# A transformer block on one core: GpSimd's additions cut by tile, the last stage's second products and the first attention's statistics moved

## The chip, the cores and the metric

The kernel runs on one core of a Trainium2 chip. Its engines are TensorE (PE, with its weight loads as PEld), VectorE (DVE), ScalarE (ACT), GpSimd (POOL) and SyncE (SP, which issues DMAs here). The metric is the device time of one execution in microseconds; the time of a kernel is the median of its runs.

## What is computed

x is 4 x 1024 tokens of 256 features (worked on as 8 halves of 4 tiles of 128 tokens; a context of 154 tokens for each of 4 batch rows, `ctx_1024`, gives keys and values). Four residual parts follow each other:

```python
x = x + tanh(g_xattn[0]) * xattn_0(layernorm(x), ctx)   # 16 heads, projections, stablemax, bias
x = x + tanh(g_ffn[0])   * moe(layernorm(x))            # 64 experts, top 8, capacity 128, and a shared expert
x = x + tanh(g_xattn[1]) * xattn_1(layernorm(x), ctx, ctx)   # softmax, no projections
x = x + tanh(g_ffn[1])   * ffn_1(layernorm(x))          # butterfly layers around a GELU

# stablemax: s = where(x >= 0, x + 1, 1 / (1 - x)); s / sum(s)
# ffn_1, whose butterflies the kernel folds into its two weight matrices:
h = butterfly(x @ W_exp + b_exp, up_weights)
h = gelu(h + up_bias)
y = butterfly(h, down_weights) @ W_con + b_con + down_bias
```

## The kernel before, in words

x stays in SBUF for the whole program, as [128 tokens, 32 tiles, 256 features]; `half_of(h)` is a half's four tiles (4 x 256 = 1024 elements a partition). Products that need precision are made of three products of split parts (a high part and a rest: `feats`, `hidden`, `w_up_high`/`w_up_low`, `w_con_high`/`w_con_low`).

The order of the work is a plan: a list of units such as `("out", h, b, k)`. Each engine walks the same list and emits the instructions that it has for each unit (`units[...]`), so the list sets each engine's order; semaphores set when an instruction may start. There are three stages.

- First attention, `plan_first`. Score products (L797, L799, L800) and the weighing of values (L816, L821) of one half run chunk by chunk with the stablemax of ACT (L1156, L1160, L1164) and DVE (L1488). What follows a half's attention is cut into steps by `after_steps(h)` and put between the chunks of the next half, one step for each chunk: division, transposing the result (`turn_att`, PE L851), `att_feats` (ACT's copies of it out of PSUM into `row_feats`, L1125), `project_o` (bias L862, products L867), `x_add` (DVE L1509: x += gate * product), statistics of the next norm (DVE L1363, POOL L1873 and L1878), norm, transposing, gate and top 8.
- The experts. Their sums come back by indirect DMA and by `fetch` in 512 KB pieces; POOL adds them to x (`add_experts`, L1910).
- Last stage, `plan_last`. It has 20 places c for each of the 8 halves, and a ninth round (h == 8) with no attention of its own. In round h the second attention of half h runs (scores L797, exponentials L1299, weighing, transposes L1068, DVE L1789 to L1794: x += gate * attention) and `beside(h, c)` says what of half h-1's last feed-forward part stands at place c: the norm "f" at c = 2 and 5 (DVE L1363, L1372, L1408; POOL L1873, L1878), `bias_out` at 7 (POOL L1914: x += the output bias), `turn_f` at 8 (PE L743; ACT L1125 and DVE L1814 make `feats`), and two bursts b = 0 and 1 at c = 9 and 13. A burst is four `up` units (PE L1085, 6 matmuls each; ACT's GELU L1328 into `hidden_whole`, of which there are two; DVE's cast L1822 and POOL's subtraction L1920 split it) and four `out` units k at c, c+1, c+2 and c+3 (PE L1100, 12 matmuls each, into two PSUM banks). Behind k = 3 stands DVE's `out_add` (L1834, two instructions of 512 elements): x += gate * products. `beside(h, 6)` also has `add_experts` for half h+2, and score maxima (`peak`, PE L1032, DVE L1774) of later halves run in between.

`out_biased` counts the bias additions, `out_added` the instructions of `out_add` (four a half), `hid_split` the subtractions. Before the change, DVE's `out_add` of burst 0 waits for `out_biased`. Exponential and GELU have different tables on ACT; a change of table is an ACT_TABLE_LOAD.

Of the kernel before, what the change touches and what calls it, by code (L numbers as in the profile page):

```python
# [14 lines left out]
ALU = mybir.AluOpType  # L15
# [3 lines left out]
P = 128  # L19
BATCH, SEQ, DIM = 4, 1024, 256  # L20
# [150 lines left out]

def after_steps(h):
    turn, divide = [("normalize", h, t) for t in range(HT)], [("divide", h, t) for t in range(HT)]
    return [turn[0:2], divide[0:2] + turn[2:4], divide[2:4], [("turn_att", h)], [("att_feats", h)],
            [("project_o", h, 0), ("project_o", h, 1)], [("x_add", h, 0), ("x_add", h, 1)],
            [("stats", "r", h), ("rstd", "r", h)], [], [("norm", "r", h)], [("turn_rows", h)], [("row_feats", h)],
            [("gate", h)], [("shift", h)], [("gate_exp", h)], [("top", h)], [("pick", h)], [("pick_rows", h), ("count", h)],
            [("position", h)]]

# [157 lines left out]

BURST_AT = (9, 13)


def peak_units(h, c):

# [5 lines left out]
def burst(h, b, peak):  # L348

    up = [("up", h, BURST * b + k) for k in range(BURST)]  # L350
    peak = peak + [None] * (4 - len(peak))
    units = [up[0], up[1], peak[0], up[2], peak[1], up[3], peak[2], ("out", h, b, 0), peak[3]]
    return [u for u in units if u]


def beside(h, c):


    units, peak = [], []
    if h + 1 < HALVES:  # L360
        peak += peak_units(h + 1, c)
    if h + 2 < HALVES:
        peak += peak_units(h + 2, c - PER_HALF)
        if c == 0:
            units.append(("fetch", h + 2))
        if c == 6:
            units += [("add_experts", h + 2, i) for i in range(SUMS)]
        if c == 10:
            units += norm_units("q1", h + 2)[:2]
        if c == 11:  # L370
            units += norm_units("q1", h + 2)[2:]
        if c == 12:
            units.append(("turn_q1", h + 2))
        if c == 13:
            units += [("send_q1", h + 2, 0), ("send_q1", h + 2, 1)]
        if c in (16, 19):
            units.append(("send_q1", h + 2, 2 + c // 19))
    if h % 2 == 0 and h + 2 < HALVES:
        b = h // 2 + 1
        if c == 1:  # L380
            units += [("load_k1", b, 0), ("load_k1", b, 1)]
            if h:
                units.append(("load_v1", b))
        if c in KEYS_AT:
            n = KEYS_AT.index(c)
            units.append(("key_split1", b, n))
            if n < 2:
                units.append(("load_k1", b, n + 2))
    if 1 <= h <= HALVES:
        if c == 2:  # L390
            units += norm_units("f", h - 1)[:2]
        if c == 5:
            units.append(norm_units("f", h - 1)[2])
        if c == 7:
            units.append(("bias_out", h - 1))
        if c == 8:
            units.append(("turn_f", h - 1))
        for b, at in enumerate(BURST_AT):
            if c == at:
                return units + burst(h - 1, b, peak)  # L400
            if at < c < at + BURST:
                units.append(("out", h - 1, b, c - at))
    return units + peak


# [68 lines left out]
def build(nc, D, out):  # L474
    ctx = ExitStack()
    with ctx:
# [882 lines left out]
        def vector_program(V):  # L1359
# [464 lines left out]
            def out_add(h, b, k):  # L1824
                if k == BURST - 1:
                    n = 2 * h + b
                    if b == 0:
                        V.wait_ge(out_biased, h + 1)
                    V.wait_ge(out_made, BURST * (n + 1))
                    for two in range(HT // 2):  # L1830
                        xs = x[:, HT * h + 2 * two:HT * h + 2 * two + 2, :].rearrange("p i f -> p (i f)")
                        if b:
                            V.wait_ge(out_added, 2 * n - 1 + two)
                        V.scalar_tensor_tensor(xs, out_bank[two], tg[:, 3:4], xs, ALU.mult,  # L1834
                                               ALU.add).then_inc(out_added, 1)
# [21 lines left out]
        def gpsimd_program(G):  # L1857
# [43 lines left out]
            def add_experts(h, i):  # L1901
                if h:
                    G.wait_ge(fetched_in[i], 16 * h)
                    if h >= HALVES - LATE:
                        G.wait_ge(*late.freed(("sh_down", h, 1)))
                    if i:
                        G.wait_ge(x_added, SUMS * (h - 1) + i)
                    elif h == 1:
                        G.wait_ge(keys_split, BATCH + 4)
                    G.tensor_tensor(half_of(h), half_of(h), fetched[i][:, :, :], ALU.add).then_inc(x_added, 1)  # L1910

            def bias_out(h):
                G.wait_ge(ln_normed, HT * (norm_no["f", h] + 1))
                G.tensor_tensor(half_of(h), half_of(h), b_out[:, :].unsqueeze(1).to_broadcast([P, HT, DIM]),  # L1914
                                ALU.add).then_inc(out_biased, 1)

            def hidden_rest(h, k):
                n = HB * h + k
# [361 lines left out]
```

## Time and profile before

| | |
|---|---|
| median of 3 runs | 1219.74 us (1217.71 to 1219.98) |
| the profiled execution | 1221.16 us, span 1219.4 us, mean granted clock 0.929 |
| busy, share of the span | PE 85%, PEld 62%, DVE 67%, ACT 58%, POOL 29% |
| chain that ended last | PE 50%, DVE 25%, ACT 11%, issue 5%, DMA 3%, POOL 3% |
| costliest parts of the chain | PE L914 6%, L1100 6%, L1085 5%, L930 4%, L1003 4%; DVE L1363 3% |

"Span" is the part of the execution that the trace covers. A granted clock of 1.00 is 2.4 GHz for TensorE, one of 0.50 is 1.2 GHz. In a row of the timeline, the number in brackets is the engine's idle time ahead of the instruction and what ended it. The first attention runs from about 40 to 350 us, the experts until about 770, the last stage from there to the end.

### The profile page before, as it was taken

What the parts mean: (1) busy time and instruction counts of PE and PEld (TensorE: products, weight loads), DVE (VectorE), ACT (ScalarE), POOL (GpSimd) and SP (SyncE); (2) the same over time, 40 slices, a digit from 0 to 9 for tenths busy, and PEclk for the clock granted to TensorE, in tenths of its full rate; (3) what the DMA queues carried; (4) which work ended last, traced back from release to release, by engine and by line L of the source; (5) the groups of instructions that cost most, each with busy time, mean ns of one, the idle gap of its engine ahead of it and who ended that gap; (6) DMA issues with size and microseconds to landing.
All of it is one profiled execution on the core that took longest, in us unless ns stands there. A gap on an engine that the chain in (4) does not pass through costs nothing.

```text
span 1219.4 us, 17480 instructions
## 1 busy us (share of the span) xinstructions
PE 1032.5 (85%) x5635; PEld 752.1 (62%) x5635; DVE 812.7 (67%) x2053; ACT 702.0 (58%) x1351; POOL 356.6 (29%) x313
## 2 busy tenths in 40 slices
PE   3888888788876788999899977889898989999878
PEld 2444544454434677877688756657676766767657
DVE  4668777877787756755657566786677677665443
ACT  2999988888965424564654431365554545444532
POOL 2000000000000003777767721233424152523223
PEclk9898988988878889999999995799999999999988
DMA  6645435442121423888888653331322233110000
GB/s 157 177 91 169 121 94 148 141 119 73 53 108 35 147 91 84 185 210 212 227 191 182 142 137 74 98 97 26 107 55 72 61 90 97 37 48 1 20 18 18
DMA packets 97435, 128.42 MB, mean 105 GB/s; under 512 B 27009, under 2 KB 69377, under 8 KB 97089
## 3 DMA queue, kind: packets, MB, share of 16 engines
q1 hardware_dynamic: 82960, 106.32, 30.6%
q0 software_dynamic: 12288, 18.88, 8.7%
q10 hardware_dynamic: 2096, 2.10, 0.8%
q8 instruction: 46, 0.75, 0.3%
q14 instruction: 45, 0.36, 0.1%
HBM read 66.15 MB, written 30.70 MB: 79 GB/s over the span
## 4 chain that ended last, share of the span: by engine, by line
PE 50%; DVE 25%; ACT 11%; issue 5%; DMA 3%; POOL 3%; SPq 2%; ACTq 1%; DVEq 0%; POOLq 0%
PE psum L914 6%; PE psum L1100 6%; PE psum L1085 5%; PE psum L930 4%; PE psum L1003 4%; DVE stats L1363 3%; PE psum L821 3%; PE psum L797 3%; PE psum L867 3%; PE psum L1032 2%; DVE weights L1488 2%; DVE peaks L1774 2%; PE psum L743 2%; ACT weights L1160 2%; PE psum L962 2%
## 5 line engine op out<-in xcount | busy, mean ns | idle before, releaser
L1873 POOL TENSOR_SCALAR vareps<-moments 128x4 f32<-128x4 f32 x32 | 10.4, 324 | 509.8 <-DVE moments L1372 509.8
L797 PE MATMUL psum<-q_stack,k_stack 96*128 96x512 f32 (+1 forms) x256 | 122.6, 508 | 33.2 <-DVE weights L1488 19.0
L1299 ACT ACTIVATE weights<-psum 128x512 f32<-128x512 f32 x160 | 94.0, 596 | 72.5 <-PE psum L797 61.1
L1488 DVE SCALAR_TENSOR_TENSOR weights<-psum,weights 128x512 f32<-128x512 f32 x160 | 102.6, 681 | 37.8 <-ACT weights L1164 37.6
L1893 POOL DMA_INDIRECT expert_sums<-made,sum_rows x64 | 103.2, 1613 | 61.5 <-DVE made L1738 37.7
L1032 PE MATMUL psum<-k_stack,q_stack 96*128 96x256 f32 x256 | 88.4, 397 | 33.0 <-DVE peaks L1774 21.5
L1920 POOL TENSOR_TENSOR hidden<-hidden_whole,hidden 128x512 fp32r<-128x512 f32 x64 | 82.2, 1286 | 115.9 <-DVE hidden L1822 115.9
L1774 DVE TENSOR_REDUCE peaks<-psum 128x2 f32<-128x308 f32 x256 | 107.2, 470 | 11.4 <-PE psum L1034 11.0
L914 PE MATMUL psum<-feat_parts,w_shared_up 128*128 128x512 f32 x384 | 99.1, 408 | 7.2 <-ACT shared_silu L1211 2.8
L1100 PE MATMUL psum<-w_con_high,hidden 128*128 128x256 f32 x512 | 101.7, 297 | 0.0
L1822 DVE CAST hidden<-hidden_whole 128x512 fp32r<-128x512 f32 x64 | 50.3, 787 | 73.8 <-ACT hidden_whole L1328 72.6
L1885 POOL DMA_INDIRECT got<-rows_scratch,tokens x64 | 68.3, 1067 | 97.1 <-DVE sum_rows L1725 77.9
L1156 ACT ACTIVATE weights<-psum 128x512 f32<-128x512 f32 x160 | 88.7, 596 | 11.4 <-PE psum L797 11.4
L1160 ACT ACTIVATE weights<-weights 128x512 f32<-128x512 f32 x160 | 94.1, 635 | 1.0
L1164 ACT ACTIVATE weights<-weights 128x512 f32<-128x512 f32 x160 | 93.9, 632 | 1.0
L797 PEld LDWEIGHTS psum<-q_stack,k_stack 96*128 96x128 f32 (+1 forms) x256 | 50.3, 201 | 71.1 <-issue 41.0
L1085 PE MATMUL psum<-feats,w_up_high 128*128 128x512 f32 x256 | 83.0, 423 | 11.6 <-DVE feats L1814 6.6
L1032 PEld LDWEIGHTS psum<-k_stack,q_stack 96*128 96x128 f32 x256 | 53.5, 209 | 61.1 <-DVE peaks L1774 28.6
L1100 PEld LDWEIGHTS psum<-w_con_high,hidden 128*128 128x128 f32 x512 | 80.9, 190 | 13.8 <-POOL hidden L1920 6.8
L914 PEld LDWEIGHTS psum<-feat_parts,w_shared_up 128*128 128x128 f32 x384 | 72.2, 194 | 23.3 <-DVE shared_silu L1612 3.6
L1328 ACT ACTIVATE hidden_whole<-psum,hidden_bias 128x512 f32<-128x512 f32 x64 | 42.7, 686 | 64.8 <-PE psum L1085 58.0
L1003 PEld LDWEIGHTS psum<-got_t,expert_w 128*128 128x128 f32 x512 | 64.2, 191 | 25.4 <-ACT got_t L1263 18.1
(211 smaller groups left out, 2416.2 us busy)
## 6 DMA issues: line engine op xcount, KB each, us to landing
expert_w<-in_expert_w SPq DMA_DIRECT2D x64, 384.0 KB, 4.2
q_stack<-q_stage SPq DMA_DIRECT2D x96, 128.0 KB, 2.9
q_stack<-q_stage SPq DMA_DIRECT2D x174, 64.0 KB, 2.0
expert_sums<-zeros SPq DMA_DIRECT2D x6, 1408.0 KB, 8.3
fetched<-expert_sums SPq DMA_DIRECT2D x14, 512.0 KB, 4.7
rows_scratch<-rows SPq DMA_DIRECT2D x8, 640.0 KB, 3.4
k_raw<-in_k SPq DMA_DIRECT2D x16, 300.0 KB
x<-in_x SPq DMA_DIRECT2D x8, 512.0 KB, 4.9
```

Of the source, the lines that this page charges most:

```text
L797: T.matmul(to, k[0:row, head_at(head), :], q[0:row, head // 2, :], start=True, stop=True).then_inc(scored, 1)
L914: m = T.matmul(shared_banks(h).ap(key, half), w_sgu[:, pw, a:a + P], sh_parts[:, pf, c * HALF:(c + 1) * HALF], start=n == 0 and c == 0, st ...
L1003: m = T.matmul(bank[2][:, part * P:(part + 1) * P], expert_w[e % 8][:, c, part * INNER:(part + 1) * INNER], got_t[e % 3][:, c, :], start=c ...
L1032: T.matmul(view[:, :, 0:P], q[0:STACK, p, t * P:(t + 1) * P], keys[0:STACK, 2 * p:2 * p + 2, :], start=True, stop=True)
L1085: m = T.matmul(wide.ap(key), up_parts[pw][:, c, k * P:(k + 1) * P], feats[:, pf, c, :], start=i == 0 and c == 0, stop=i == 2 and c == CD - 1)
L1100: m = T.matmul(out_bank[t // 2][:, t % 2 * DIM:(t % 2 + 1) * DIM], hidden[k][:, ph, t * P:(t + 1) * P], con_parts[pw][:, BURST * b + k, :] ...
L1160: A.activation(weights[n % 9][:, :], weights[n % 9][:, :], ACT.Ln, bias=1.0).then_inc(logged, 1)
L1164: A.activation(weights[n % 9][:, :], weights[n % 9][:, :], ACT.Exp, scale=-1.0).then_inc(exped, 1)
L1299: A.activation(weights1[n % 6][:, :], score_bank[n % 2], ACT.Exp).then_inc(exped, 1)
L1488: V.scalar_tensor_tensor(weights[n % 9][:, :], score_bank[n % 5], 1.0, weights[n % 9][:, :], ALU.add, ALU.max).then_inc(weighted, 1)
L1774: V.tensor_reduce(peaks[h % 2][:, t, 2 * p:2 * p + 2], view, AX.X, ALU.max).then_inc(wide.frees(key, i), 1)
L1893: G.indirect_dma_start(sum_dram[e % SUMS], bass.IndirectOffsetOnAxis(ap=sum_rows[:, e:e + 1], axis=0), made[e % 4][:, :], None, bounds_che ...
```

## The change

Four things are changed.

1. POOL's additions to x, of the experts' sums and of the output bias, are made tile by tile: four instructions of 128x256 for each of 128x1024. The semaphore is counted once, by the last of the four.
2. `bias_out` moves from c = 7, where it waited for the norm, to c = 12, where it waits for both instructions of `out_add` of the first burst. `out_add` of the second burst now waits for it, and that of the first no longer does.
3. The second burst's `out` units of half 6, (6, 1), are kept out of round 7's places 13 to 16 and put at places 2, 2, 5 and 5 of the ninth round, behind the norm units of those places.
4. `after_steps`: an empty step comes before `att_feats`, and `x_add` and the statistics of the norm become one step, so everything behind keeps its place.

```diff
-    return [turn[0:2], divide[0:2] + turn[2:4], divide[2:4], [("turn_att", h)], [("att_feats", h)],
-            [("project_o", h, 0), ("project_o", h, 1)], [("x_add", h, 0), ("x_add", h, 1)],
-            [("stats", "r", h), ("rstd", "r", h)], [], [("norm", "r", h)], [("turn_rows", h)], [("row_feats", h)],
+    return [turn[0:2], divide[0:2] + turn[2:4], divide[2:4], [("turn_att", h)], [], [("att_feats", h)],
+            [("project_o", h, 0), ("project_o", h, 1)],
+            [("x_add", h, 0), ("x_add", h, 1), ("stats", "r", h), ("rstd", "r", h)], [], [("norm", "r", h)], [("turn_rows", h)], [("row_feats", h)],
...
+KEPT_BACK, KEPT_BACK_AT = (HALVES - 2, 1), (2, 2, 5, 5)
...
-    units = [up[0], up[1], peak[0], up[2], peak[1], up[3], peak[2], ("out", h, b, 0), peak[3]]
+    first = None if (h, b) == KEPT_BACK else ("out", h, b, 0)
+    units = [up[0], up[1], peak[0], up[2], peak[1], up[3], peak[2], first, peak[3]]
...
-        if c == 7:
+        if c == 12:
             units.append(("bias_out", h - 1))
...
-            if at < c < at + BURST:
+            if at < c < at + BURST and (h - 1, b) != KEPT_BACK:
                 units.append(("out", h - 1, b, c - at))
+        if h == HALVES:
+            units += [("out", *KEPT_BACK, k) for k in range(BURST) if c == KEPT_BACK_AT[k]]
...
-                    if b == 0:
+                    if b:
                         V.wait_ge(out_biased, h + 1)
...
-                    G.tensor_tensor(half_of(h), half_of(h), fetched[i][:, :, :], ALU.add).then_inc(x_added, 1)
+                    for t in range(HT):
+                        xt = x[:, HT * h + t, :]
+                        m = G.tensor_tensor(xt, xt, fetched[i][:, t, :], ALU.add)
+                    m.then_inc(x_added, 1)

             def bias_out(h):
-                G.wait_ge(ln_normed, HT * (norm_no["f", h] + 1))
-                G.tensor_tensor(half_of(h), half_of(h), b_out[:, :].unsqueeze(1).to_broadcast([P, HT, DIM]),
-                                ALU.add).then_inc(out_biased, 1)
+                G.wait_ge(out_added, 4 * h + 2)
+                for t in range(HT):
+                    xt = x[:, HT * h + t, :]
+                    m = G.tensor_tensor(xt, xt, b_out[:, :], ALU.add)
+                m.then_inc(out_biased, 1)
```

The changed program's lines are numbered 5 higher up to the additions, and 10 to 16 higher behind them. Its order on the engines differs at these places.

PE, first attention, around one half's `project_o` (L862 and L867, after the change L867 and L872), before:

```order
L816 MATMUL psum<-weights,values 128x512
L851 MATMUL psum<-ident,att 128x128 x8
L797 MATMUL psum<-q_stack,k_stack 128x512 x2
L862 MATMUL psum<-bias_parts,bias_ones 128x512
L867 MATMUL psum<-wo,row_feats 128x256 x4
L862 MATMUL psum<-bias_parts,bias_ones 128x512
L867 MATMUL psum<-wo,row_feats 128x256 x4
L797 MATMUL psum<-q_stack,k_stack 128x512 x2
L821 MATMUL psum<-weights,values 32x512 x4
L799 MATMUL psum<-q_stack,k_stack 128x512
L800 MATMUL psum<-q_stack,k_stack 128x512
```

and after:

```order
L821 MATMUL psum<-weights,values 128x512
L856 MATMUL psum<-ident,att 128x128 x8
L802 MATMUL psum<-q_stack,k_stack 128x512 x4
L826 MATMUL psum<-weights,values 32x512 x4
L867 MATMUL psum<-bias_parts,bias_ones 128x512
L872 MATMUL psum<-wo,row_feats 128x256 x4
L867 MATMUL psum<-bias_parts,bias_ones 128x512
L872 MATMUL psum<-wo,row_feats 128x256 x4
L804 MATMUL psum<-q_stack,k_stack 128x512
L805 MATMUL psum<-q_stack,k_stack 128x512
L821 MATMUL psum<-weights,values 128x512
L802 MATMUL psum<-q_stack,k_stack 128x512 x2
```

The four score products stand together, and with the four weighing products in front of `project_o`, where two score products stood before.

POOL, last stage, around one half's bias addition, before:

```order
L1920 TENSOR_TENSOR hidden<-hidden_whole,hidden 128x512 x4
L1873 TENSOR_SCALAR vareps<-moments 128x4
L1878 TENSOR_TENSOR rstd<-vareps,minus_half 128x4
L1914 TENSOR_TENSOR x<-x,bias_out 128x1024
L1920 TENSOR_TENSOR hidden<-hidden_whole,hidden 128x512 x8
```

and after:

```order
L1878 TENSOR_SCALAR vareps<-moments 128x4
L1883 TENSOR_TENSOR rstd<-vareps,minus_half 128x4
L1930 TENSOR_TENSOR hidden<-hidden_whole,hidden 128x512 x4
L1924 TENSOR_TENSOR x<-x,bias_out 128x256 x4
L1930 TENSOR_TENSOR hidden<-hidden_whole,hidden 128x512 x4
```

The addition leaves the place behind the reciprocal deviation (L1878) for the one between the two bursts' subtractions.

DVE, from the last attention's `x` updates of half 7 to `feats`, before:

```order
L1834 SCALAR_TENSOR_TENSOR x<-psum,tanh_gates,x 128x512 x2
L1789 RECIPROCAL sums_0<-psum 128x16
L1791 TENSOR_TENSOR att_0<-psum,sums_0 128x256
L1794 SCALAR_TENSOR_TENSOR x<-att_0,tanh_gates,x 128x4x64
L1789 RECIPROCAL sums_1<-psum 128x16
L1791 TENSOR_TENSOR att_1<-psum,sums_1 128x256
L1794 SCALAR_TENSOR_TENSOR x<-att_1,tanh_gates,x 128x4x64
L1363 BN_STATS stats<-x 128x6 x4
L1372 BN_AGGR moments<-stats 128x2 x4
L1408 TENSOR_SCALAR normed<-x,moments,rstd 128x256 x4
L1814 TENSOR_TENSOR feats<-psum,feats 128x512 x2
```

and after:

```order
L1827 CAST hidden<-hidden_whole 128x512 x4
L1794 RECIPROCAL sums_0<-psum 128x16
L1796 TENSOR_TENSOR att_0<-psum,sums_0 128x256
L1799 SCALAR_TENSOR_TENSOR x<-att_0,tanh_gates,x 128x4x64
L1794 RECIPROCAL sums_1<-psum 128x16
L1796 TENSOR_TENSOR att_1<-psum,sums_1 128x256
L1799 SCALAR_TENSOR_TENSOR x<-att_1,tanh_gates,x 128x4x64
L1368 BN_STATS stats<-x 128x6 x4
L1377 BN_AGGR moments<-stats 128x2 x4
L1413 TENSOR_SCALAR normed<-x,moments,rstd 128x256 x4
L1839 SCALAR_TENSOR_TENSOR x<-psum,tanh_gates,x 128x512 x2
L1819 TENSOR_TENSOR feats<-psum,feats 128x512 x2
```

The update of x by (6, 1) (L1834, L1839) moves behind the last normalisation. On PE the 48 products of (6, 1) move likewise: they now stand between the last transposes of the attention (L1068, L1073) and those of `turn_f` (L743, L748).

## Rows read from the trace of the kernel before

**Rows 1.** Windows: stretch, length, busy time of each engine (instructions), clock.

```profile
779.00:793.00 14.00, 13.21 (x50) 8.66 (x48) 10.46 (x28) 5.52 (x10) 2.10 (x3) 0.51 0.22 38
...
1182.00:1196.00 14.00, 8.53 (x23) 6.48 (x24) 5.00 (x16) 3.85 (x5) 4.37 (x4) 0.51 0.00 0
```

**Rows 2.** Waits, first attention: engine, line <- line: total, times, longest us.

```profile
ACT row_feats L1125 <- PE psum L851: 14.6, 5, 3.6
```

**Rows 3.** POOL's groups: count, busy us, mean ns, idle before and releasers.

```profile
L1878 POOL TENSOR_TENSOR rstd<-vareps,minus_half 128x4 f32<-128x4 f32 x32 | 33.2, 1037 | 4.6
L1910 POOL TENSOR_TENSOR x<-x,fetched 128x1024 f32<-128x1024 f32 x14 | 33.2, 2370 | 53.2 <-DMA fetched<-expert_sums 43.7 <-DVE k_stack L1758 8.5 <-POOL x L1910 0.2
```

**Rows 4.** Timeline, half 6: start, us, engine, line, [idle before].

```profile
1142.65 2.38 POOL L1914 TENSOR_TENSOR x<-x,bias_out 128x1024 f32<-128x1024 f32 x1 [1.57 <-DVE normed L1408]
...
1143.24 2.08 DVE L1794 SCALAR_TENSOR_TENSOR x<-att,tanh_gates,x 128x256 f32<-128x256 f32 x1
...
1146.62 0.70 PE L1085 MATMUL psum<-feats,w_up_high 128*128 128x512 f32 x2 [2.00 <-DVE feats L1814]
```

**Rows 5.** Timeline, half 5, the same place.

```profile
1093.62 1.29 DVE L1814 TENSOR_TENSOR feats<-psum,feats 128x512 fp32r<-128x512 f32 x2 [0.36 <-ACT feats L1125]
...
1095.01 0.47 PE L1085 MATMUL psum<-feats,w_up_high 128*128 128x512 f32 x1 [0.45 <-issue]
```

**Rows 6.** Chain of waits, last two halves: start, us, what.

```profile
1146.62 7.36 PE psum L1085 x24
...
1189.67 8.62 PE psum L1085 x24
...
1203.98 5.55 PE psum L1085 x24
1209.54 5.70 PE psum L1100 x48
```

**Rows 7.** Timeline, half 2.

```profile
930.09 0.70 PE L1085 MATMUL psum<-feats,w_up_high 128*128 128x512 f32 x2 [1.51 <-DVE feats L1814]
```

**Rows 8.** Timeline, ahead of the last stage's halves, DVE.

```profile
775.54 2.37 DVE L1794 SCALAR_TENSOR_TENSOR x<-att,tanh_gates,x 128x256 f32<-128x256 f32 x1
```

**Rows 9.** Timeline, half 0, POOL and DVE.

```profile
814.33 4.93 POOL L1910 TENSOR_TENSOR x<-x,fetched 128x1024 f32<-128x1024 f32 x2 [4.39 <-DMA fetched<-expert_sums]
...
819.22 2.57 POOL L1914 TENSOR_TENSOR x<-x,bias_out 128x1024 f32<-128x1024 f32 x1
...
819.79 2.28 DVE L1822 CAST hidden<-hidden_whole 128x512 fp32r<-128x512 f32 x1 [0.24 <-ACT hidden_whole L1328]
```

**Rows 10.** Timeline, half 0, between the two bursts.

```profile
839.16 1.40 DVE L1834 SCALAR_TENSOR_TENSOR x<-psum,tanh_gates,x 128x512 f32<-128x512 f32 x2
...
842.54 1.28 POOL L1920 TENSOR_TENSOR hidden<-hidden_whole,hidden 128x512 fp32r<-128x512 f32 x1 [8.27 <-DVE hidden L1822]
...
844.38 0.69 ACT L1328 ACTIVATE hidden_whole<-psum,hidden_bias 128x512 f32<-128x512 f32 x1 [1.87 <-PE psum L1085]
```

**Rows 11.** Timeline, half 7, between the two bursts.

```profile
1204.09 1.41 DVE L1834 SCALAR_TENSOR_TENSOR x<-psum,tanh_gates,x 128x512 f32<-128x512 f32 x2 [3.98 <-PE psum L1100]
...
1206.78 1.29 POOL L1920 TENSOR_TENSOR hidden<-hidden_whole,hidden 128x512 fp32r<-128x512 f32 x1 [5.30 <-DVE hidden L1822]
...
1211.73 1.29 POOL L1920 TENSOR_TENSOR hidden<-hidden_whole,hidden 128x512 fp32r<-128x512 f32 x1 [0.36 <-DVE hidden L1822]
```

**Rows 12.** Timeline, first attention, half 0, ACT.

```profile
86.21 1.09 ACT L1156 ACTIVATE weights<-psum 128x512 f32<-128x512 f32 x2 [1.62 <-PE psum L797]
```

**Rows 13.** Timeline, first attention, PE and ACT beside one row_feats.

```profile
205.68 1.16 PE L816 MATMUL psum<-weights,values 128*128 128x512 f32 x2
...
207.40 1.08 ACT L1125 ACTIVATE row_feats<-psum 128x512 f32<-128x512 f32 x2 [3.37 <-PE psum L851]
```

**Rows 14.** Timeline, PE ahead of the last transposes.

```profile
1186.01 2.21 PE L743 MATMUL psum<-ident,normed 128*128 128x128 f32 x8 [5.16 <-DVE normed L1408]
```

**Rows 15.** Timeline, ACT in the last attention.

```profile
1169.87 1.28 ACT L1299 ACT_TABLE_LOAD   x1
```

## The prediction

> **What bounds the kernel now.** I read the busy shares first: PE 85% of the span, DVE 67%, ACT 58%, POOL 29%, with the granted clock at 9 tenths in most slices. So PE is the engine to feed, and POOL's own time counts only where somebody waits for it. Then I took the stretches in which the clock falls to half. The reader should see two long ones, 14 us each, at clock 0.51 [rows 1]: one behind the first additions of the last stage, one around the last normalisation. Then the timeline just ahead of each, to find who was late. In both, and in most short stalls of that stage, the chain is: POOL works on x with 128x1024 elements, DVE's small update of x stretches beside it, the split of `feats` comes late, PE's `up` products come late. In the first attention I read the table of waits; there the one row on this change is ACT's wait for the transposes that it copies, 14.6 us in 5 times [rows 2].
>
> The profiled execution took 1221.16 us (span 1219.4), 1.4 above the median of the runs, 1219.74. I sum against 1221.2 and subtract 1.4 at the end.
>
> **A. The additions by tile (14 by experts, 8 of the bias): gain 9.5.** An addition of 1024 elements takes 2.37 us [rows 3]. In half 6, the bias addition ran from 1142.65 to 1145.03; DVE's 256-element update started at 1143.24 and took 2.08 us, to its end [rows 4]. Where nothing of POOL's lies beside it the same form takes some 0.48. The engine that starts first keeps the other waiting until its instruction ends. So PE's `up` started after 2.00 us idle [rows 4], against 0.45 in half 5, where DVE had 0.36 to spare [rows 5]: 1.55. Its 24 matmuls then took 7.36 us, where 24 at full clock take about 5.55 [rows 6]; 1.8 more, of which I take 1.45, since a slice of the clock's fall may remain. Half 6 gives 3.0. In three earlier halves the addition of experts meets the same update; PE's idle time there was 1.51 [rows 7], and 1.69 and 0.54 in the same row of the next two: 1.1 + 1.2 + 0.1 = 2.4. At 775.54 the update took 2.37, 1.9 more than alone [rows 8], and the half-clock stretch [rows 1] follows: 1.9 and, of the clock, 1.0, as much of these 14 us is bound by DVE (busy 10.46): 2.9. At 814 two additions (4.93) and the bias addition behind them (2.57, from 819.22) hold POOL, and DVE's cast takes 2.28 [rows 9] where it takes 0.43 alone. Afterwards eight slices (5.95) and two casts between them (0.86) take 6.8 against 7.5, 0.7, with 0.5 for the clock behind it: 1.2.
>
> What a slice costs is not in the trace. POOL's 128x512 form takes 1.28 to 1.29 [rows 10, 11], its 1024 form 2.37: 1.08 for 512 elements and 0.20 fixed, so 0.20 + 0.54 = 0.74 for 256. The bounds are 0.59 (a quarter of 2.37) and 1.29 (not below the 512 form); I take 0.74. Four slices are 2.98, 0.6 longer than one addition, but DVE can get between two of them, and then waits 0.74 at most and 0.37 on average, about the 0.36 it can spare.
>
> The row of 1143.24 shows a block, not a slowing of both. The Trainium skill, "SBUF — State Buffer", section "Who interferes with whom", says the same: DVE and GpSimd share a port pair, and the first to issue holds it for its whole instruction. Its rule speaks against the change too, as the lock works both ways: DVE's casts between two slices hold up POOL. By that the four bias slices would take up to 2.98 + 3 x 0.43 = 4.3; this is the price used under B, which rests on the rows of the casts.
>
> **B. The bias addition behind the first burst's update: loss 5.9.** It leaves the place before `turn_f` and waits for DVE's update by the first burst; POOL then cannot start the second burst's subtractions. The gap between that update's end and the first subtraction is its cover. The first of the eight, half 0: 840.56 to 842.54, 1.98 [rows 10]. The last, half 7: 1205.50 to 1206.78, 1.28 [rows 11]. Between them, by the same two rows of each half, 2.0, 3.0, 2.0, 3.0, 3.0, 3.0. The bias needs 3.0 and a start of 0.1, and a cast (0.43) gets in now and then. Three halves at 2.0: 3.1 + 0.5 - 2.0 = 1.6 late. The third GELU of half 0 started at 844.38 for PE, while the subtraction that frees its buffer had ended at 843.82 [rows 10], so 0.56 is hidden; 1.0 to 1.1 each, 3.3. Halves at 3.0: 0.25 each for three, 0.75; half 6, where the exponentials of the last attention queue behind the GELUs, 0.65. Half 7: POOL 1.9 late; the fourth subtraction would end at 1214.9 instead of 1213.02 [rows 11], and PE wants it for the last 12 of the 48 products that start at 1209.54 and take 5.70 [rows 6], at 1209.54 + 3 x 1.43 = 1213.8: 1.2. Sum 5.9. Bounds: 0, if PE's other work covers all; and 8 x 3.1 = 24.8, if the gaps are filled by nothing useful and the addition stands on the path in full. I stay near the rows with gaps. DVE's second update now waits for the bias, but its products end many us later; nothing.
>
> **C. First attention: gain 1.9.** Per half, two score products more and four of the weighing come ahead of `project_o`. ACT fed by them no longer idles 1.62 us ahead of 86.21 [rows 12]: 1.6 in half 0. In the other halves, ACT copies `row_feats` one clip later, and its wait ends with the weighing at 206.84 (205.68 + 1.16) instead of at the copy, 207.40 [rows 13]: 0.5 sooner, but `project_o` and so DVE's x_add and statistics come some 1.2 us later, and the next transposes take most of it back; 0.05 each, 0.3. Bounds: 14.6 if the whole row of waits goes [rows 2]; -3.5 if in seven halves the later statistics cost 0.5 each. I stay near the lower part, because PE (busy 85%) must do the same products.
>
> **D. The tail: gain 3.5.** 48 `out` products of half 6 leave the last attention groups. There they took four pieces of 1.43 or more; now they stand in PE's idle 5.16 us [rows 14] before `turn_f`. Without them the attention is bound by ACT, whose table load starts at 1169.87 [rows 15], and ends about 1.65 sooner (six exponentials and two copies at 0.6, then the last weighing, 2.1, and its copy: 1178.5 against 1180.14). The moved products then run from 1179.2 to 1184.9, and `turn_f` starts there instead of at 1186.01: 1.1 sooner. PE doesn't cool: the 24 matmuls at 8.62 [rows 6] cost 5.55, 3.1 more. That makes 4.2; I take 3.5, as the thinner attention tail may cost some clock. Bounds: 4.2, and -1 if the products run at the clock of the 14 us at 0.51 [rows 1]. DVE's update of (6, 1) moves behind the normalisation, where DVE is idle; nothing.
>
> **Sum.** 9.5 - 5.9 + 1.9 + 3.5 = 9.0; 1221.2 - 9.0 = 1212.2; less 1.4, 1210.8, told as 1211.
>
> **Rivals.**
> 1. *C is larger.* ACT's waits in the first attention go by half, 7.3 instead of 1.9: about 5.5 more, 1205.5. For it: the wait is one cause in 5 places. Against: PE has the same work there.
> 2. *The tail cools.* Taking 48 products out of the last attention thins PE's work; the clock falls there, the moved products take up to twice 5.7 us and `turn_f` is late. D goes from 3.5 to about -0.5: 1215. For it: PE fell to 0.51 in this very stretch [rows 1]. The Trainium skill, "TensorE: Matmul & The Clock Gate", section "HAM oscillation — how this bites in real kernels", describes short pieces of matmuls between waits that run cold each time; it would make this rival the forecast.
> 3. *Stalls change hands.* DVE waits for slices four times where it waited once, A shrinks to about 2: 1218.5, within the bound of no change.
> 4. *Slower: the slice.* 32 bias slices stand behind the first burst's update, in gaps that are full. Each us that a slice costs beyond 0.74 adds up to 32 us; 9 us of gain are gone at 0.74 + 9/32 = 1.0. At 1.2 (near the 128x512 row) 14.7 are lost: 1226. For it: POOL's 128x4 form of the same kind takes 1.04 [rows 3], so the fixed part may depend on operands. Against: two sizes of plain additions give 0.20 fixed.
>
> **Chances.** Forecast 0.50 (its own range 1207.5 to 1214.5); rival 1 0.14; rival 2 0.16; rival 3 0.09; rival 4 0.11. About 0.2% (2.4 us) is what a measurement of this kernel tells from no change. Forecast, rival 1, and nearly all of rival 2 are faster: 0.78; rival 3 and a rest of 2 are the same: 0.13; rival 4, less a little, slower: 0.09. The range 1204.5 to 1219 takes in rivals 1 to 3 and leaves out 4 and the far ends of C.
>
> **What would show it.** A: DVE's update of x never over 1.2 us in the last stage, PE's idle before `up` about 0.5; slices near 0.74. B: between update and first subtraction 3.0 to 3.6 us in each half. C: the wait of ACT at 86 gone. D: no idle over 2 us before the last `turn_f`, and the next 24 matmuls in 5.6. The forecast is wrong if slices take 1 us or more, if the clock in the last 50 us stays near half, or if halves 0, 1 and 3 of the last stage grow by more than 2 us each.

## The result

| | before | after |
|---|---|---|
| median | 1219.86 us (1217.71 to 1222.35, 4 runs) | 1237.83 us (1236.55 to 1238.79, 4 runs) |
| profiled execution's span | 1219.4 us | 1236.0 us |
| mean granted clock | 0.929 | 0.911 |

The changed kernel is slower: ratio 1.0127, interval 1.0100 to 1.0154. The forecast was 1211 us, range 1204.5 to 1219. It was wrong in sign.

### The profile page after: what moved, and what is told of

Its sections match the earlier page's. It is cut to its first block, busy times and chain, and to the rows that moved or that the text cites. A ratio compares the mean times of both kernels' runs of the same rounds, so it can differ in the third digit from the quotient of the medians.

```text
span 1236.0 us, 17538 instructions
## 1 busy us (share of the span) xinstructions
PE 1052.7 (85%) x5635; PEld 765.1 (62%) x5635; DVE 801.9 (65%) x2053; ACT 702.9 (57%) x1351; POOL 371.0 (30%) x379
## 4 chain that ended last, share of the span: by engine, by line
PE 54%; DVE 24%; ACT 9%; issue 5%; POOL 3%; SPq 2%; DMA 2%; ACTq 1%; DVEq 0%; POOLq 0%
PE psum L919 6%; PE psum L1105 5%; PE psum L1090 5%; PE psum L1008 4%; PE psum L826 4%; PE psum L935 4%; PE psum L802 4%; DVE stats L1368 3%; PE psum L872 3%; DVE weights L1493 3%; DVE peaks L1779 2%; PE psum L748 2%; PE psum L821 2%; PE psum L1037 2%; PE psum L967 2%
## 5 line engine op out<-in xcount | busy, mean ns | idle before, releaser
L1878 POOL TENSOR_SCALAR vareps<-moments 128x4 f32<-128x4 f32 x32 | 10.4, 324 | 526.5 <-DVE moments L1377 526.5
L802 PE MATMUL psum<-q_stack,k_stack 96*128 96x512 f32 (+1 forms) x256 | 125.9, 525 | 47.1 <-DVE weights L1493 30.4
L1827 DVE CAST hidden<-hidden_whole 128x512 fp32r<-128x512 f32 x64 | 45.2, 711 | 80.7 <-ACT hidden_whole L1333 79.6
L1090 PE MATMUL psum<-feats,w_up_high 128*128 128x512 f32 x256 | 80.2, 410 | 13.6 <-ACT hidden_whole L1333 8.7
L1008 PEld LDWEIGHTS psum<-got_t,expert_w 128*128 128x128 f32 x512 | 66.8, 198 | 24.6 <-ACT got_t L1268 14.8
L826 PE MATMUL psum<-weights,values 128*32 128x512 f32 x512 | 80.9, 707 | 1.1 <-ACT turned L1176 1.1
```

The costliest lines, as they stand in the source:

```text
L802: T.matmul(to, k[0:row, head_at(head), :], q[0:row, head // 2, :], start=True, stop=True).then_inc(scored, 1)
L826: m = T.matmul(to[32 * j:32 * j + 32, :], vals[:, 0, 4 * g + j, :], w[(n + j) % len(w)][:, :], start=True, stop=False, tile_position=(0, 3 ...
L1008: m = T.matmul(bank[2][:, part * P:(part + 1) * P], expert_w[e % 8][:, c, part * INNER:(part + 1) * INNER], got_t[e % 3][:, c, :], start=c ...
L1090: m = T.matmul(wide.ap(key), up_parts[pw][:, c, k * P:(k + 1) * P], feats[:, pf, c, :], start=i == 0 and c == 0, stop=i == 2 and c == CD - 1)
```

## The profile after

First, where the time went. I cut both traces at instructions that both have: the reciprocal deviations of the norms, which POOL computes (L1878, after the change L1883). The 16th, at the end of the first attention, starts at 375.1 us before and at 393.6 after: 18.5 late. The 18th, shortly ahead of the last stage, is 21.3 late; the end of the span 16.6. So the last stage gained 4.7, the forecast's A, B and D together, and the loss is in the first attention, the forecast's smallest term. (The other 2.8 us between the two cuts are in the experts' stage, whose length differs between the traces of all kernels by 6 us.) The lateness grows from half to half, at the deviations of the norm behind each half's attention: 0.9, 4.0, 5.4, 6.6, 11.3, 12.9, 15.3 and 18.5.

The stretch from 40 us to that deviation by the windows (length, then busy time of PE, PEld, DVE, ACT, POOL with instructions, granted clock, DMA share, GB/s). Before:

```profile
40.00:375.10 335.10, 279.02 (x1274) 155.35 (x1272) 256.82 (x735) 289.72 (x559) 16.78 (x28) 0.90 0.40 112
```

After:

```profile
40.00:393.70 353.70, 297.37 (x1279) 166.90 (x1278) 258.08 (x735) 291.05 (x559) 16.86 (x28) 0.84 0.38 106
```

Subtract the busy time from the length. PE's idle time is 335.1 - 279.0 = 56.1 before and 353.7 - 297.4 = 56.3 after. It did not wait longer; it was busy 18.4 us longer with the same instructions. DVE and ACT did the same work within 1.4 us of the same time. What changed is the clock, 0.90 to 0.84. In windows of half a microsecond, PE was at 1.2 GHz (a clock under 0.75) for 68 us before and 110 after; by my estimate 42 us more at half speed cost about 21 us, near the 18.4. In six traces with the old steps (before, e1, e5, e6, e9, f1) this time is 58 to 73.5 us and PE's busy time 275.8 to 283.3, so the change stands clear of the scatter.

The wait that the prediction counted on [rows 2] did go, and another came. Waits from 40 to 350 us, the stretch of [rows 2], before:

```profile
PE psum L797 <- DVE weights L1488: 19.0, 18, 2.2
```

and after:

```profile
PE psum L802 <- DVE weights L1493: 28.6, 23, 2.2
...
ACT turned L1176 <- PE psum L821: 21.4, 10, 3.3
DVE x L1514 <- PE psum L872: 18.4, 13, 1.7
```

ACT's 14.6 us for `row_feats` are not in the answer any more; its wait for the weighing, 4.5 us in 4 times before, is 21.4 in 10. Much of it is the same idle time under the name of the next instruction in the queue, as half 3 shows. After, against [rows 13]:

```profile
210.84 1.02 PE L821 MATMUL psum<-weights,values 128*128 128x512 f32 x2
211.70 1.03 PE L856 MATMUL psum<-ident,att 128*128 128x128 f32 x8
211.96 0.60 ACT L1176 ACTIVATE turned<-psum 128x512 f32<-128x512 f32 x1 [2.48 <-PE psum L821]
```

ACT starts 1.12 us behind the start of the weighing, where it was 1.72: 0.6 sooner, as forecast (0.5); its idle time fell from 3.37 to 2.48. What follows a few microseconds behind that place is shown by half 2, before:

```profile
172.50 1.07 PE L821 MATMUL psum<-weights,values 128*32 128x512 f32 x8
...
174.54 1.25 DVE L1488 SCALAR_TENSOR_TENSOR weights<-psum,weights 128x512 f32<-128x512 f32 x2
...
175.25 1.10 PE L797 MATMUL psum<-q_stack,k_stack 96*128 96x512 f32 x2 [0.17 <-DVE weights L1488]
```

and after:

```profile
177.59 0.75 DVE L1514 SCALAR_TENSOR_TENSOR x<-psum,tanh_gates,x 128x512 f32<-128x512 f32 x1 [1.60 <-PE psum L872]
...
178.38 1.40 DVE L1368 BATCH_NORM_STATS2 stats<-x 128x6 f32<-128x256 f32 x4
...
179.98 1.26 DVE L1493 SCALAR_TENSOR_TENSOR weights<-psum,weights 128x512 f32<-128x512 f32 x2
...
180.69 1.09 PE L802 MATMUL psum<-q_stack,k_stack 96*128 96x512 f32 x2 [1.82 <-DVE weights L1493]
...
182.26 2.20 PE L748 MATMUL psum<-ident,rows 128*128 128x128 f32 x8 [0.47 <-DVE rows L1413]
```

DVE did the same in this piece before as after: its second x_add, the statistics and the weights follow each other, and the weights start 2.39 us behind the x_add (172.15 to 174.54, and 177.59 to 179.98). PE's next scores overwrite what the weights read, so they wait for them. What changed is PE's own work beside that: two scores and the weighing of the row at 172.50, about 1.7 us, stood behind `project_o` before and have been pulled in front of it. PE idles 1.82 us where it idled 0.17 before. The transposes of the norm, 1.64 us in the same place before, take 2.20. The windows show the fall. Before, at the same place:

```profile
176.00:180.00 4.00, 3.43 (x19) 1.51 (x19) 3.74 (x10) 3.94 (x9) 0.12 (x1) 1.00 0.00 0
```

and after:

```profile
174.00:178.00 4.00, 4.00 (x18) 3.06 (x17) 1.27 (x3) 4.00 (x9) 0.00 (x0) 1.00 0.00 0
178.00:182.00 4.00, 1.87 (x5) 0.41 (x3) 3.50 (x12) 3.94 (x8) 1.26 (x2) 1.00 0.00 0
182.00:186.00 4.00, 3.74 (x14) 2.10 (x18) 4.00 (x15) 2.85 (x6) 0.04 (x1) 0.65 0.04 12
```

Four full microseconds, four with PE busy for 1.87, then a clock of 0.65. Half 0 shows the exchange in small: ACT's idle 1.62 [rows 12] is gone, and PE pays 1.81 behind it:

```profile
85.79 1.07 ACT L1161 ACTIVATE weights<-psum 128x512 f32<-128x512 f32 x2
...
89.92 1.10 PE L802 MATMUL psum<-q_stack,k_stack 96*128 96x512 f32 x2 [1.81 <-DVE weights L1493]
```

The last stage went mostly as forecast. The slices, against [rows 3]:

```profile
L1917 POOL TENSOR_TENSOR x<-x,fetched 128x256 f32<-128x256 f32 x56 | 40.1, 746 | 49.0 <-DMA fetched<-expert_sums 39.5 <-DVE k_stack L1763 8.5 <-POOL x L1917 0.2
...
L1924 POOL TENSOR_TENSOR x<-x,bias_out 128x256 f32<-128x256 f32 x32 | 25.4, 824 | 45.4 <-DVE x L1839 45.4
```

0.746 us for a slice, forecast 0.74; those of the bias take 0.82, with DVE's casts beside them. Half 6 without its stall, against [rows 4]:

```profile
1164.16 0.48 DVE L1799 SCALAR_TENSOR_TENSOR x<-att,tanh_gates,x 128x256 f32<-128x256 f32 x1
1166.00 0.70 PE L1090 MATMUL psum<-feats,w_up_high 128*128 128x512 f32 x2 [0.45 <-issue]
```

And the last two halves by the chain of waits, against [rows 6]:

```profile
1166.00 5.79 PE psum L1090 x24
...
1206.53 7.34 PE psum L1090 x24
```

7.36 became 5.79, 8.62 became 7.34. The moved bias in half 7, against [rows 11]:

```profile
1219.61 1.41 DVE L1839 SCALAR_TENSOR_TENSOR x<-psum,tanh_gates,x 128x512 f32<-128x512 f32 x2 [3.18 <-PE psum L1105]
...
1221.10 3.19 POOL L1924 TENSOR_TENSOR x<-x,bias_out 128x256 f32<-128x256 f32 x4 [3.29 <-DVE x L1839]
...
1224.26 2.52 POOL L1930 TENSOR_TENSOR hidden<-hidden_whole,hidden 128x512 fp32r<-128x512 f32 x2
```

The first subtraction starts 3.24 us behind the update's end, 1.28 before. Over the eight halves these gaps are 3.01, 4.05, 3.25, 4.05, 3.25, 3.23, 3.26 and 3.24, where they were 1.98, 2.00, 3.01, 2.01, 3.01, 2.99, 3.00 and 1.28. Two of them lie above the 3.0 to 3.6 that the prediction gave for each half.

## The experiments

Each kernel was timed against the kernel before on its chip. The medians of the kernel before lie between 1219.86 and 1223.05 on these chips, so compare ratios and not medians. The columns: median; ratio with its 95% interval; from one trace each, the start of the 16th deviation (the first attention's end) and the length of the last stage, from the 18th deviation to the end of the span.

| | median | ratio | first attention ends | last stage |
|---|---|---|---|---|
| before | 1219.86 | 1 | 375.1 | 476.3 |
| after | 1237.83 | 1.0127 (1.0100, 1.0154) | 393.6 | 471.6 |
| e1_old_steps | 1219.18 | 0.9977 (0.9952, 1.0002) | 373.2 | 469.2 |
| e2_steps_only | 1243.79 | 1.0194 (1.0160, 1.0228) | 393.6 | 476.4 |
| e3_late_apart | 1236.24 | 1.0118 (1.0088, 1.0147) | 396.3 | 473.8 |
| e4_joined_early | 1223.69 | 1.0030 (1.0001, 1.0059) | 379.2 | 473.5 |
| e10_copies_late | 1229.78 | 1.0078 (1.0043, 1.0113) | 385.0 | 474.2 |
| e11_products_late | 1232.00 | 1.0081 (1.0046, 1.0116) | 387.8 | 478.8 |
| e12_late_packed | 1242.14 | 1.0163 (1.0097, 1.0229) | 396.2 | 476.1 |
| e14_early_products | 1239.95 | 1.0152 (1.0098, 1.0206) | 393.4 | 473.2 |
| e13_one_half | 1226.40 | 1.0023 (0.9998, 1.0047) | 380.0 | 473.6 |
| e5_tiles | 1217.51 | 0.9977 (0.9956, 0.9998) | 376.7 | 469.8 |
| e6_kept_back | 1221.72 | 0.9995 (0.9962, 1.0028) | 376.7 | 471.4 |
| e7_bias_whole | 1223.07 | 1.0013 (0.9993, 1.0034) | 379.1 | 473.8 |
| e8_tiles_kept | 1216.81 | 0.9959 (0.9922, 0.9996) | 377.0 | 469.0 |
| e9_experts_kept | 1215.21 | 0.9958 (0.9940, 0.9976) | 372.8 | 472.5 |
| e16_kept_moved | 1215.77 | 0.9943 (0.9918, 0.9969) | 377.0 | 468.8 |
| f1_old_steps_again | 1219.31 | 0.9967 (0.9943, 0.9991) | 378.9 | 468.9 |
| f9_experts_kept_again | 1214.57 | 0.9951 (0.9928, 0.9974) | 374.7 | 467.3 |
| f16_kept_moved_again | 1214.44 | 0.9944 (0.9924, 0.9963) | 376.6 | 465.6 |

How far one trace can be trusted: eleven have the old first attention, and it ends between 372.8 and 379.1, mean 376.2. Nine have the old last stage, 473.2 to 478.8, mean 475.1.

In the listings below each bracket is one step of `after_steps`; the units are written short.

**Which edit costs.** The steps undone in the changed kernel, and alone on the kernel before:

```diff
 # e1_old_steps: on the changed kernel; e2_steps_only: on the kernel before, with - and + exchanged
-    [("turn_att", h)], [], [("att_feats", h)], [project_o 0 and 1], [x_add 0 and 1, stats, rstd], [], [("norm", "r", h)]
+    [("turn_att", h)], [("att_feats", h)], [project_o 0 and 1], [x_add 0 and 1], [stats, rstd], [], [("norm", "r", h)]
```

> The changed kernel with the first attention's steps as they were before; the slices, the moved bias and the products kept back stay. If the whole loss is the first attention's (in the trace of the changed kernel it is 18.6 us late at the last x_add of that stage, 21.4 late at the start of the last stage, and 16.8 late at the end), this runs in about 1219.9 - 4.6 = 1215. If the last stage's edits also move something ahead of them, or the late start only gave slack back, 1219 to 1222.

> The kernel before with the new steps of the first attention and nothing else. If these steps are the loss: 1219.9 + 21 = 1241, slower than the changed kernel by the 4.6 that its last stage gains. If the loss needs the other edits: within 1 us of 1220.

The steps alone are 1.94% slower and end the first attention at 393.6, where the changed kernel does. Without them the rest is 0.23% faster, with an interval that reaches no change (0.33% in the repetition, clear of it); the 1215 that I expected of e1 was not reached. The loss is the steps'. The difference of 1.94% and 1.27% would leave 0.67% for the other edits, where e1 and its repetition read 0.23% and 0.33%; the intervals overlap.

**Joined, or late.** The two parts of the edit, apart from each other:

```diff
-    [turn_att], [att_feats], [project_o], [x_add], [stats, rstd], [], [norm]
 # e3_late_apart: all behind turn_att one step later
+    [turn_att], [], [att_feats], [project_o], [x_add], [stats, rstd], [], [norm]
 # e4_joined_early
+    [turn_att], [att_feats], [project_o], [x_add, stats, rstd], [], [], [norm]
```

> The kernel before with the empty step ahead of att_feats alone; x_add and the statistics stay two steps, so all that follows comes one step later. Theory 'joined' (DVE works on x_add and statistics in one piece, PE's next scores wait for DVE's weights, the clock falls): little loss, 1218 to 1224. Theory 'late' (the copies one step later are the loss): 1234 or more.

> The kernel before with x_add and the statistics joined in one step, one step after project_o, at its old place; a second empty step keeps the rest in place. Theory 'joined': most of the loss, 1232 to 1240, with PE idle about 1.8 us ahead of the scores behind each second statistics. Theory 'late': 1220 +- 2. If both are needed, both this and the run before are near 1220 and only the pair costs 21.

My favourite, "joined", fell: joining costs 0.3%, and its first attention ends at the upper edge of the old steps' range. Being late costs 1.2%. But that loss is of another form: from 40 to 396.2 us, e3's PE is idle 14.5 us more than before and busy only 6.6 more; in e3 the norm too comes a step later. I then asked which instruction's lateness it is:

```diff
-    [turn_att], [att_feats], [project_o], [x_add], [stats, rstd], [], [norm]
 # e10_copies_late
+    [turn_att], [], [att_feats, project_o], [x_add], [stats, rstd], [], [norm]
 # e11_products_late
+    [turn_att], [att_feats], [], [project_o], [x_add, stats, rstd], [], [norm]
 # e12_late_packed
+    [turn_att], [], [att_feats], [project_o], [x_add], [stats, rstd], [norm]
```

> The kernel before with att_feats alone one step later, so in front of project_o in project_o's old step; x_add, statistics and all behind stay. Separates the later copies from the later products. Theory 'copies': the old wait only changes its name from row_feats to turned, cost 3 us or more, 1224+. Theory 'chain' (project_o, x_add and statistics come late against a norm that stays, and PE has short pieces and idles at the norm): 1219 to 1223.

> The kernel before with att_feats at its old step, project_o one step later and x_add and statistics joined behind it, the norm in place. Theory 'chain': nearly the whole loss, 1234 to 1244, all of it as time at half clock in the first attention. Theory 'copies': 1220 to 1225.

> The kernel before with copies, project_o, x_add and statistics each one step later and apart, and the empty step between statistics and norm used up, so the norm and all behind it stay. If what costs is that DVE does x_add and statistics in one piece: 1222 to 1230, better than the joined 1243. If it is their lateness against the norm: 1236 or more, with DVE waiting for the deviations.

Each alone costs about 0.8%, where all the new steps cost 1.9%; theory "copies" and theory "chain" are each half right. (e11 also joins x_add and the statistics, as the new steps do.) At the place of half 2 shown above PE idles 1.82 us ahead of its scores in e11, which has PE's new order, and 0.16 in e4 and e10, which keep the old one. So this gap comes with PE's order, and joining on DVE does not make it. The same window of e11 and of e12:

```profile
40.00:388.00 348.00, 289.41 (x1280) 162.90 (x1278) 258.01 (x735) 291.47 (x560) 16.98 (x28) 0.86 0.38 108
```

```profile
40.00:396.20 356.20, 285.85 (x1274) 160.70 (x1272) 257.57 (x737) 291.06 (x560) 16.81 (x28) 0.85 0.38 106
```

e11: idle 58.6 (2.5 more than before), busy 10.4 more, so four fifths of its loss is clock. e10, to 384.8 us: idle 5.0 more, busy 4.7 more, half and half. e12: idle 70.4 (14.3 more), busy 6.8 more; its statistics stand right in front of the norm, and in half 2 PE idles 3.23 us ahead of the norm's transposes and not at all ahead of the scores. e12 thus costs nearly as much without joining, but mostly in waits. The lateness can be paid in either form.

**Direction, and a single half.**

```diff
-    [turn_att], [att_feats], [project_o], [x_add], [stats, rstd], [], [norm]
 # e14_early_products
+    [turn_att], [att_feats, project_o], [x_add], [stats, rstd], [], [], [norm]
 # e13_one_half
+    if h == 4: [turn_att], [], [att_feats], [project_o], [x_add, stats, rstd], [], [norm]
```

> The kernel before with project_o, x_add and statistics one step earlier than before, the norm in place: the opposite move. If lateness against the fixed norm is what costs, earliness costs nothing or gains: 1216 to 1221. If any move of project_o from behind the two score products costs: 1226 or more, as PE then waits for ACT's copy of the transposes.

> The kernel before with the new steps in one half of the first attention (half 4, where the changed kernel loses most, 4.7 us) and the old ones in the other seven. Theory 'clock by half' (each half pays for itself by PE running longer at half clock): about 4 to 5 us late behind half 4 and no more after it, 1224 to 1226. Theory 'chain' (a delay that is carried on from half to half): it grows behind half 4, or the loss needs all halves and this is 1220 to 1222.

The move the other way costs as much, 1.5%. "Late against a fixed norm" is therefore not the cause, or not all of it. Waits of e14 in its first attention (40 to 395 us):

```profile
DVE x L1508 <- PE psum L866: 39.2, 16, 4.5
```

(The first step of ACT's stablemax, L1155, waits for PE's scores 22.0 us in 13 times there.) Here `project_o` stands on PE ahead of scores that ACT needs, and waits for its copies. Its window:

```profile
40.00:393.30 353.30, 292.58 (x1270) 161.00 (x1268) 255.76 (x733) 289.17 (x558) 16.77 (x27) 0.86 0.38 107
```

Idle 60.7, 4.6 more than before; busy 13.6 more. Again most is clock. One half's new steps cost 0.23% by the times (-0.02% to 0.47%, so not clear of nothing). Against the trace of before, and counted from the halves ahead, it is 1.7 us late at that half's deviation, 2.7 and 5.2 at the next two, and 5.2 at the end of the stage. So in this one trace a half's disturbance is paid within the next two halves and isn't amplified from there on. Eight times the 2.8 us of its times would be 22, near the loss of e2; eight times 5.2 would be 42, so single halves don't simply add up, or this trace overstates one.

**The last stage's edits.**

```diff
 # e5_tiles: on the kernel before; add_experts likewise
-                G.tensor_tensor(half_of(h), half_of(h), b_out[:, :].unsqueeze(1).to_broadcast([P, HT, DIM]), ...
+                for t in range(HT):
+                    m = G.tensor_tensor(x[:, HT * h + t, :], x[:, HT * h + t, :], b_out[:, :], ALU.add)
 # e6_kept_back
+KEPT_BACK, KEPT_BACK_AT = (HALVES - 2, 1), (2, 2, 5, 5)
 # e7_bias_whole: one instruction, with the places of out_biased's waits as in the change
-        if c == 7:
+        if c == 12:
-                G.wait_ge(ln_normed, HT * (norm_no["f", h] + 1))
+                G.wait_ge(out_added, 4 * h + 2)
 # e8_tiles_kept: e5 and e6. e9_experts_kept: e6 and e5's add_experts. e16_kept_moved: e9 and e7.
```

> The kernel before with all additions by tile, the bias at its old place. My term A: 5 to 9.5 us less, so 1211 to 1215, with no update of x by DVE over 1.3 us in the last stage. Rival: DVE waits for several slices instead of once and the gain is under 2 us, 1218 to 1221.

> The kernel before with the second products of half 6 kept back behind the last norm, nothing else. By the trace of the changed kernel (from 21.0 us late at half 6's transposes to 17.2 at the last norm, 16.8 at the end): 3.5 to 4.3 us less, 1217. If the tail's gain needs the moved bias: under 1.5.

> The kernel before with the bias addition behind the first burst's update, in one piece of 1024 elements (2.4 us, waits the same), no slices. My term B: the move costs 4 to 7 us and gives back the stalls that the addition caused before the turn (3.0 in half 6, 0.7 + 0.5 in half 0, and in half 2, 3 and 4 it was the experts' addition, which stays): net 1 to 4 us slower, 1221 to 1224. Rival: the gap covers it in one piece, net 2 us faster.

> Additions by tile at their old places and the products kept back, without the moved bias and without the new steps: the best that my terms give, A + D = 9 to 13 us less, 1207 to 1211. If slices give nothing: 1216 to 1217.

> As the run before, but the bias addition stays one of 1024 elements: only the experts' additions are by tile. By A the bias slices are worth 3.0 (half 6) + 1.2 (half 0): 3 to 4 us slower than the run before, 1211 to 1214. If sliced bias costs POOL time that shows, this is the faster of the two.

> The kernel before with the experts' additions by tile, the products kept back, and the bias addition in one piece behind the first burst's update. A for the experts (5), D (3.6 by the trace of the run with it alone), and for the moved whole bias 0 to 2 gained (its trace: 2.4 less in the last stage, its times within 0.3% of before): 1210 to 1215. If the moved bias costs what I forecast under B: 1217 to 1220.

Tiles alone are 0.23% faster, with a last stage of 469.8, 5.3 under the mean of 475.1. e5 and e8 stayed behind what my terms gave (1211 to 1215 and 1207 to 1211). e9 was expected 3 to 4 us slower than e8, as its bias is whole; by its times it is no slower (ratios 0.9958 and 0.9959), so slicing the bias gains nothing that these times show. In the trace of e6 the `up` products behind the last normalisation cost 5.78 us for 24, and from the 31st deviation to the end it takes 76.1, where nine old tails take 77.5 to 79.3, mean 78.4: 2.3 less. By its times e6 is not told from the kernel before. e7 is within noise. The chain of waits of e6:

```profile
1146.59 5.80 PE psum L1090 x24
...
1188.44 5.78 PE psum L1090 x24
```

Its first row also warns of single traces: in half 6 DVE's update took 2.07 beside the whole bias addition and PE idled 1.98 ahead of its `up` products, as before, and yet these took 5.80, where they took 7.36 before. Three versions were timed again beside each other on one chip:

> The changed kernel with the old steps again, now beside the two best versions on one chip. By the traces of the last stage (7.3 us less than the kernel before from the stage's start): 0.3 to 0.6% below before. By the first timing: 0.2%.

> Experts' additions by tile, products kept back, bias whole at its old place. First timing 0.42% below before. If the moved whole bias is worth something, this is 1 to 3 us slower than the next.

> As the run before with the bias moved in one piece. First timing 0.57% below before, its gap between update and subtraction 2.8 to 3.6 us. If the slices of the bias cost what the gaps say (0.2 us a half, 0.5 in two), this is 1 to 2 us faster than the changed kernel with the old steps.

All three beat the kernel before. The best is the experts' additions by tile, the products kept back and the bias moved in one piece, over the old steps: 1214.44 us, 0.56% below before (0.37% to 0.76%), where the changed kernel is 1.27% above it. Between it, f9 and f1 the intervals overlap, so that the bias is better in one piece is suggested and not shown.

## Why the prediction was wrong

- **C is the step that failed:** "the next transposes take most of it back; 0.05 each", with a lower bound of -3.5. By the traces it is -18.5; by the times of the steps alone, 1.94%, about -23. I had each row right: ACT's 1.62 in half 0 went, its wait in half 3 ended sooner, x_add and statistics came 1.0 to 1.6 us later behind `turn_att` in halves 1 to 6. But the next transposes took nothing of that back: in these six halves they start 12.5, 11.3, 12.5, 11.3, 11.3 and 12.0 us behind `turn_att` before and 13.5, 12.4, 14.0, 12.4, 12.9 and 13.1 after, 1.0 to 1.6 later each, 7.4 in sum. And I priced the lateness by waits alone and left the clock out, although I used the clock in A and D. And the argument I put against a larger effect, "PE must do the same products", holds for their number and not for their duration: the same products took 18.4 us longer with the same idle time. What went wrong in the bound: it took 0.5 us a half, the wait saved, as the scale of the loss too. The trace of before showed twelve stretches at half clock between 40 and 375 us, 68 us in sum. That was the sign that the clock falls often in this stage, and the sum had no term for it. That the gaps like the one of half 2 make the added stretches is argued from their order in the trace; no run filled a gap to see.
- The Trainium skill's section "HAM oscillation — how this bites in real kernels" in "TensorE: Matmul & The Clock Gate" describes matmuls in short pieces between waits that run cold again and again. The trace shows the like in the first attention, with the difference that the page's waits are for DMA and this one is of 1.82 us for DVE. I looked for it in the wrong stage: rival 2 put it into the tail. There the 48 products between the last transposes ran at full clock (0.28 us a matmul), and only the `up` products behind were partly slow, 7.34.
- **A** was right in mechanism: the slices at 0.746, no attention update of x over 0.91 in the changed kernel's last stage, `up` behind 0.45. Of the size, 9.5 forecast, 5.3 measured (e5's trace) and 0.23% by the times, 2.8 us; the parts at half 6 (3.0) measured 2.1 in the tail of e5 (76.3 against 78.4), and the times of e8 and e9 show nothing for the slices of the bias. It was over-sized because it added up stalls of one trace, and the 7.36 of half 6 isn't there in every trace of the same instructions.
- **B** was over-sized too, 5.9 against about 1: the changed last stage (469.2, 468.9, 471.6, mean 469.9) against the same without the move (e8, 469.0, one trace). The gaps on POOL grew by 8.1 us in sum, about as worked out (in two halves by 2.0 instead of 1.6; the sum used 3.6 for addition and cast together and not the 4.3 that A's last paragraph names). By the difference, PE rarely had to wait for them; which of its other work covered them was not traced half by half. Half 7, the one place without cover, was right: 25.4 us from the `up` products to the last update where it had been 25.6, with 1.3 saved by the clock, so 1.1 lost; forecast 1.2.
- **D** came out near its size in the trace: 3.5 forecast, 2.3 by e6's tail and 3.7 by its whole last stage. By e6's times it can't be told from nothing, so it is suggested and not shown.
- The sum of A, B and D, 7.1, came out as 4.7 in the trace of the changed kernel and 0.23% to 0.33% in the times of e1 and f1, 3 to 4 us. That it is near is luck in part: two errors of 4 and 5 us of opposite sign met in it.
- **The rivals.** The slower one, that a slice costs 1 us or more, did not occur. The rival that did, that the first attention's new order costs clock, wasn't among them; the chance of 0.09 for slower was all on the wrong mechanism.

What stays open: why exactly 0.8% for the copies alone, how the loss of one half adds up to that of eight, and whether a constant work for PE in the gap behind the statistics would keep the clock up. That was not tried.

## What to carry to other kernels

- Price a reordering of a stage by the clock as well as by waits. Where a stage already drops to half clock again and again, a wait moved from another engine onto PE can cost slow products behind it beside the wait itself (here 18.4 us of busy time at equal idle time); compare PE's busy time at equal work, and its idle time, before believing either.
- Where a stage is interleaved by hand, both neighbours of the present place can be worse (here 0.8% to 1.9% in either direction). A wait that ends sooner on ACT says nothing about the end unless PE gets its next operands sooner.
- Test each part of a bundle alone: of four edits here three together gave 0.2% to 0.3% (0.6% in the best form, with the bias in one piece), and the fourth took 1.9%.

## What the runs showed of the hardware

- The same products in the same stretch of the program took 279.0 us of PE's time at a mean granted clock of 0.90 and 297.4 at 0.84, with idle times of 56.1 and 56.3 us. The sum of the idle time alone thus does not tell the clock. PE was busy for 4.00 us of 4, then for 1.87 of 4 with no single idle over 1.82 us, and then ran at a clock of 0.65.
- POOL's addition takes 0.746 us for 256 elements, its subtraction 1.29 for 512, its addition 2.37 for 1024: an estimate of 0.20 us fixed and 1.08 for 512 elements fits all three. Where DVE's casts run beside it, a slice takes 0.82.
- A DVE update of 256 elements takes 0.48 us alone. Beside an addition of POOL's it ran until that ended: up to 2.37 us beside 1024 elements; in the changed kernel, with slices, none took over 0.91.
